# Gated cross-attention and mixture-of-experts block on one core: second matmul of FFN passes 2 to 4 as half-precision pairs, with the order of the weight splits and the place of one buffer changed

## The reference

```python
logits = xf @ gate_w + gate_b
top_w, top_i = jax.lax.top_k(logits, K)                     # K = 2 of E = 8
gw = jax.nn.softmax(top_w, axis=-1)
combine = (gw[:, :, None] * one_hot(top_i, E)).sum(axis=1)
for e in range(E):
    h = gelu(xf @ w1[e] + b1[e])                            # 128 -> 512
    out = out + combine[:, e:e + 1] * (h @ w2[e] + b2[e])   # 512 -> 128
shared = gelu(xf @ ws1 + bs1) @ ws2 + bs2
x = x + tanh(g_ffn) * (out + shared)
```

## Time and profile before

| | |
|---|---|
| median of three runs | 154.49 us |
| profiled execution, its own time | 153.82 us |
| its span | 151.8 us |
| PE busy | 140.6 us (93%) |
| POOL busy | 118.7 us (78%) |
| ACT busy | 114.7 us (76%) |
| DVE busy | 101.6 us (67%) |
| granted TensorE clock, mean | 0.999 |

### The profile page before, as it was taken

How to read it: one execution, slowest core, us unless ns; L and a number is a source line. 1 busy time by engine, 2 the same in 40 slices (tenths; PEclk the granted TensorE clock), 3 DMA queues, 4 the chain that set the end, 5 groups by cost and what they waited for, 6 DMA issues and landing times.

```text
span 151.8 us, 4483 instructions
## 1 busy us (share of the span) xinstructions
PE 140.6 (93%) x1844; PEld 108.3 (71%) x1844; DVE 101.6 (67%) x215; ACT 114.7 (76%) x191; POOL 118.7 (78%) x104
## 2 busy tenths in 40 slices
PE   7779699979899999999989789999999999999992
PEld 4434354537566666657778579999999998999992
DVE  0779898879777688876873184353768785865631
ACT  3556789998987988889658989195579899768720
POOL 6506999779999798998999999895365589886730
PEclk9999999999999999999999999999999999999999
DMA  4679997000000000000000000050000001000001
GB/s 146 200 249 303 281 346 232 1 0 4 0 9 4 2 4 0 4 0 0 4 0 4 0 4 4 0 138 4 0 0 0 9 0 35 4 0 4 0 0 35
DMA packets 10254, 7.71 MB, mean 51 GB/s; under 512 B 1102, under 2 KB 8443, under 8 KB 10235
## 3 DMA queue, kind: packets, MB, share of 16 engines
q1 hardware_dynamic: 10234, 7.44, 16.4%
HBM read 7.18 MB, written 0.26 MB: 49 GB/s over the span
## 4 chain that ended last, share of the span: by engine, by line
PE 74%; DVE 11%; ACT 8%; issue 3%; DMA 2%; SPq 0%; DVEq 0%; ACTq 0%
PE banks L1000 13%; PE banks L1002 11%; PE banks L1001 11%; PE banks L1283 8%; DVE part L830 5%; PE banks L1179 4%; PE banks L1181 3%; PE banks L1180 3%; ACT prob L655 3%; PE banks L1129 3%; PE banks L1199 2%; PE banks L1147 2%; PE banks L1134 2%; PE banks L1139 2%; ACT v_hi L644 2%
## 5 line engine op out<-in xcount | busy, mean ns | idle before, releaser
L555 POOL TENSOR_TENSOR p_lo<-prob,p_hi 128x1024 f16<-128x1024 f32 x23 | 49.0, 2133 | 4.8 <-ACT p_hi L663 4.5
L719 ACT ACTIVATE prob<-banks,b1T 128x256 f32<-128x256 f32 x72 | 28.0, 475 | 8.5 <-PE banks L1002 8.5
L655 ACT ACTIVATE prob<-banks 128x1024 f32<-128x1024 f32 x24 | 24.5, 1022 | 8.1 <-PE banks L1147 8.1
L830 DVE TENSOR_REDUCE part<-banks 128x2 f32<-128x1024 f32 (+1 forms) x24 | 29.0, 1216 | 1.1 <-PE banks L1102 1.0
L578 POOL TENSOR_TENSOR k_both<-prob,k_both 128x1024 f16<-128x1024 f32 x11 | 23.4, 2132 | 6.6 <-ACT k_both L727 5.9
L663 ACT ACTIVATE p_hi<-prob 128x1024 f16<-128x1024 f32 x24 | 25.4, 1057 | 0.8
L1000 PE MATMUL banks<-x2h,wf 128*128 128x256 f16 x72 | 19.6, 273 | 0.0
L1002 PE MATMUL banks<-x2h,wf 128*128 128x256 f16 x72 | 19.6, 273 | 0.0
L1001 PE MATMUL banks<-x2h,wf 128*128 128x256 f16 x72 | 19.6, 272 | 0.0
L1179 PEld LDWEIGHTS banks<-v_hi,p_hi 128*128 128x128 f16 x192 | 17.4, 98 | 2.8 <-issue 2.5
L1179 PE MATMUL banks<-v_hi,p_hi 128*128 128x65 f16 x192 | 19.2, 195 | 0.0
(11 more groups left out here) (153 smaller groups left out, 345.0 us busy)
## 6 DMA issues: line engine op xcount, KB each, us to landing
ring<-in_L_ffn_w_dram SPq DMA_DIRECT2D x16, 256.0 KB, 5.0
wf<-in_ctx_dram SPq DMA_DIRECT2D x2, 256.0 KB, 5.5
ring<-in_L_xattn_Wk_dram SPq DMA_DIRECT2D x2, 256.0 KB, 4.1
ring<-in_L_xattn_Wv_dram SPq DMA_DIRECT2D x2, 256.0 KB, 6.7
ring<-in_L_ffn_ws_dram SPq DMA_DIRECT2D x2, 256.0 KB, 6.5
x_sb<-in_x_dram SPq DMA_DIRECT2D x1, 256.0 KB, 2.8
ring<-in_L_xattn_Wq_dram SPq DMA_DIRECT2D x1, 256.0 KB, 4.4
wo<-in_L_xattn_Wo_dram SPq DMA_DIRECT2D x1, 256.0 KB, 7.5
```

Source lines behind the costliest of these rows:

```text
L555: nc.gpsimd.tensor_tensor(p_lo[:, u % RINGP, :, :].rearrange("p a n -> p (a n)"), prob[:, u % RINGE, :], p_hi[:, u % RINGP, :, :].rearrang ...
L655: nc.scalar.activation(prob[:, u % RINGE, :], units(u).rearrange("p a n -> p (a n)"), ACT.Exp, scale=DH ** -0.5 / S_SCORE).then_inc(exp_do ...
L719: nc.scalar.activation(hid[:, k % NHID, c * T1:(c + 1) * T1], span(2 * (k % 2), HC * T1)[:, c * T1:(c + 1) * T1], ACT.Gelu, bias=b1T[:, e ...
L830: nc.vector.tensor_reduce(dst, src, AX_X, ALU.max).then_inc(part_done, 1)
```

## The change

Second matmuls of passes 2, 3 and 4 become pairs: `FULL32` keeps 0, 1, 8 and 17. Their second matrices, which were split at steps 30 to 33 for batch 1 alone, are split at steps 25, 26 and 27; that of place 1 stays with ACT and DVE, a step later (31 instead of 30). The second matrix of pass 7 goes from POOL to ACT and DVE (step 30), that of pass 6 stays with POOL but moves from step 25 to step 28, and the first matrix of pass 6 moves from step 25 to step 27. `oT` of batch 1 moves into the key buffer of batch 1. The wait on `y_ps` ahead of a cast is left out for a pass below HB, where nothing was to be waited for.

```diff
-POOL_W2 = (5, 6, 7)
-POOL_W2_STEP = (FFN0, FFN0 + 1, FFN0 + 2)
-W1_STEP = {5: FFN0, 6: FFN0 + 1, 7: FFN0 + 4, 8: FFN0 + 5}
-W2_STEP = {1: FFN0 + 6, 2: FFN0 + 7, 3: FFN0 + 8, 4: FFN0 + 9}
+POOL_W2 = (5, 6)
+POOL_W2_STEP = (FFN0, FFN0 + 4)
+W1_STEP = {5: FFN0, 6: FFN0 + 3, 7: FFN0 + 4, 8: FFN0 + 5}
+W2_STEP = {2: FFN0 + 1, 3: FFN0 + 2, 4: FFN0 + 3, 7: FFN0 + 6, 1: FFN0 + 7}
...
-FULL32 = [k for k in range(NE) if k not in POOL_W2] + [NF - 1]
+FULL32 = [0, 1, NE - 1, NF - 1]
 SPLIT_HID = [k for k in range(NF) if k not in FULL32]
...
-        oT = kflat.bitcast(F32)[:, 0:NT * INNER].rearrange("p (t n) -> p t n", t=NT)
+        oT = k_both[:, :, :, :, :].rearrange("p b a h n -> p b (a h n)").bitcast(F32)[:, :, 0:QT * INNER].rearrange(
+            "p b (t n) -> p b t n", t=QT)
...
                     if k in SPLIT_HID:
-                        act.wait_ge(y_ps, k - HB + 1)
+                        if k >= HB:
+                            act.wait_ge(y_ps, k - HB + 1)
...
-                    nc.vector.tensor_copy(oT[:, QT * b + s, :], tail_bank(b, s)).then_inc(misc_done, 1)
+                    nc.vector.tensor_copy(oT[:, b, s, :], tail_bank(b, s)).then_inc(misc_done, 1)
...
                 if k in SPLIT_HID:
-                    dve.wait_ge(y_ps, k - HB + 1)
+                    if k >= HB:
+                        dve.wait_ge(y_ps, k - HB + 1)
...
-                            last = nc.tensor.matmul(misc[:, q * D:(q + 1) * D], oT[:, t, cols], wo[:, cols],
+                            last = nc.tensor.matmul(misc[:, q * D:(q + 1) * D], oT[:, b, q, cols], wo[:, cols],
```

## The result

The changed kernel takes 157.29 us (median of six runs, 156.88 to 158.69) against 154.38 for the kernel before (six runs, 153.89 to 155.51): a ratio of 1.020, 95% interval 1.0158 to 1.0243. It is slower by 2.9 us, where 2.0 was forecast. The profiled execution took 158.69, its span is 156.9.

A forecast was written before the change was run, and what follows sets the result against it. TensorE (93% busy) was taken as the bound, fed by POOL's low parts. A saving of 1.35 us against four waits (0.4, 1.4, 0.3, 1.3: 3.4) gave +2.0, a median of 156.5 us; range 154.2 to 157.9.

The forecast's parts named there:

- TensorE's saving, 0.45 a pass: Second matmuls of passes 2 to 4 take 1.34 us as pairs, not 1.79; 1.35 saved if nothing waits.
- Pass 2 waits 0.4 for POOL: Second matmul of pass 2 starts at 103.8 instead of 103.38, behind POOL's subtraction from 101.6 to 103.7.
- The copies of the attention output end late, and the product with Wo waits 1.4: DVE's two `oT` copies end at 106.7 instead of 103.0; TensorE's Wo product waits from 105.4 to 106.8.
- Passes 3 and 4: Second matmul of pass 3 starts at 110.2, +1.3 at its end; that of pass 4 has no wait, ends at 114.95.
- The meetings on POOL's four small instructions, 0.3: Ahead of pass 5's subtraction, meeting DVE adds 0 to 1.5 us to POOL's 1.76; 0.3 taken, pass 5 at +2.2.
- From pass 5 on as before, less 0.2: Passes after pass 5's second matmul run as before; about 0.2 us of later waits on POOL should vanish.
- POOL meets nobody: Rival: POOL goes on before a waiting DVE gets in; no Wo product wait, 154.4, -0.1; chance 0.20.
- The saving stays: Rival: pass 5's low part lands by 114.0 and TensorE waits nowhere, 153.1; chance 0.05.
- Every meeting costs in full: Rival: waiting instructions have no time behind them, step 29's small ones each meet DVE; +3.2, 157.7; chance 0.15.
- The prediction's other sum, +3.3: By the skill page's rule, five DVE and POOL meetings cost about 1.3 us more: +3.3 instead of +2.0.
- The pair saves nothing: Rival: the three extra passes do not run at 1.34 because 24 loads go with them; 158; chance 0.03.

The follow-up runs named there:

- e11: e8 with ACT's cast of place 1's second matrix moved from step 31 to step 33; 153.21 us, ratio 0.9911 to the kernel before.
- e9: Changed kernel with 18 matmuls that nothing reads, some 2.0 us, put ahead of the second matmul of pass 5; 156.96 us, ratio 1.0187.
- e10: Changed kernel with the first matrix of pass 7 split in step 25 instead of 28; 156.68 us, ratio 1.0167.
- e1: Changed kernel with POOL's split of pass 6's second matrix back in step 25 instead of step 28; 154.24 us, ratio 0.9989.
- e8: Changed kernel with the edits of e1 and e2, pass 3's second matrix split a step earlier, pass 2 in f32; 153.80 us, ratio 0.997.
- e2: Changed kernel with DVE's two copies of the attention output ahead of its cast of pass 3; 157.91 us, ratio 1.0229.

## Why the prediction was right, and where not

The direction and the mechanism held, and 157.29 lies in the range. By its steps:

1. *TensorE's saving, 0.45 a pass*: right. e11 keeps 0.90 of 0.90 at pass 5.
2. *Pass 2 waits 0.4 for POOL*: the wait is 0.36, and the block starts 0.52 late. The other 0.16 are no idle time in the list, because it counts from the end of the last matmul, 0.27 behind its start, while without a stop the next one starts 0.11 behind it.
3. *The copies of the attention output end late, and the product with Wo waits 1.4*: right in size (listed 1.38, copies ending at 106.98), one block off in place. What waits is the gate transpose of batch 0 just ahead of it, since it writes the PSUM bank from which the second copy reads.
4. *Passes 3 and 4*: within 0.1 us.
5. *The meetings on POOL's four small instructions, 0.3*: this is the term that was mis-sized. They took 3.16 us (113.53 to 116.69) instead of 1.76, so the meetings cost 1.4, near the upper end of the bound (1.5), in a case to which the prediction gave 0.15. I had reasoned that DVE is mostly busy there with sums that read PSUM. But each low part has a cast right behind it, and POOL is held through both (0.95 and 1.08 instead of 0.22 and 0.25). Pass 5 came at +3.2 instead of +2.2.
6. *From pass 5 on as before, less 0.2*: right at full clock; pass 17 came 31.51 behind pass 5 in e9 and 31.67 before. In two of the six runs the granted clock falls, which no step of mine had: +1.5 in the profile of after.

Of the missing 0.9 us some 0.3 come from the two runs with the lower clock: the four at full clock have a median of 157.0. The other 0.6 are part of the 1.1 by which the meetings were sized too small. From profile to profile (153.82 before, 156.96 in e9) the loss is 3.1 and shows all of it: the profiled execution before was 0.6 under its median of 154.38, that of e9 was at its median.

Of the rivals, *POOL meets nobody* is refuted by the timelines and by e10: DVE even gets in between two subtractions of which the second was ready. *The saving stays* is refuted as well: pass 5's low part landed at 118.8 and not by 114.0. *Every meeting costs in full* was nearest in size (157.7), and right about the small instructions, but not about what a meeting costs a large one: POOL's split at 104.02 ended at 105.51, 0.90 behind DVE's end at 104.61, as I had taken it. The Trainium skill ("SBUF — State Buffer", Who interferes with whom) has it right that one blocks the other for a whole instruction, and the trace agrees with 2.27 instead of 0.68 for DVE's low part. The prediction's other sum, +3.3, is near the +3.23 of pass 5 by luck: by pass 4, behind the large meetings, the start was +1.37, near my +1.3, and the excess arose at the small instructions. Its 115 ns stand in the Trainium skill ("SBUF — State Buffer", A bandwidth-pool intuition that's wrong) for a DMA held up behind a VectorE copy, which no run here shows. *The pair saves nothing* is refuted by e11.

## What to carry to other kernels

When work is moved from the bound engine to helpers, add up the helper's own queue between its first new input and the date at which the bound engine asks, including what is moved into that stretch; if that sum reaches the date, the saving is gone before any contention is counted. Here 3.4 us of a weight split, moved from an idle stretch into the busy one, turned a level time (e1) into a loss of 2%. Where two helpers hold each other up, count how many instructions of one stand back to back, since even a small instruction of the other can wait for all of them (0.95 and 1.08 us here; in e8 one of 0.66 us was done between the two). And of several waits in a row only the last one that is set by the slow queue counts: taking away an earlier one moves it, as in e2.

## What was not expected of the hardware

- The granted clock of TensorE fell to 1.2 GHz (0.50 from 119.8 to 123.1, matmuls at half pace) less than 1 us after the end of a wait of 2.14 us; two of six runs of the same program show the mean clock that goes with it, and it cost 1.6 us. With the wait filled the clock stayed full in four of four runs, and with a wait of 1.54 (e10) as well. That the wait is the cause is not shown.
- A wait that the profile lists with 0.36 us delays TensorE's next block by 0.52, because matmuls overlap (0.27 long, 0.11 apart).
- Two POOL instructions that follow each other without a wait still let DVE in between: two subtractions took 4.65 us instead of 4.22, and a DVE instruction that began during the first ended 0.54 behind it (119.35 against 118.81).
